# First norm of an AdaLN block without transposes: paired statistics, rows spread through DRAM, product on GpSimd, join on VectorE

## The reference

```
mod = (silu(c) @ wmod).reshape(16, 6, 1, 256)            # sa, ca, ga, sb, cb, gb
h  = layernorm(x) * (1 + ca) + sa                          # first norm, over channels
x  = x + ga' * attention(h)                                # a state-space layer
h  = layernorm(x) * (1 + cb) + sb                          # second norm
x  = x + gb' * feedforward(h)

attention: u, gate = split(h @ W_in.T);  b = u @ W_state.T
           dt = min(softplus(u @ W_dt.T + b_dt), 10);  decay = exp(-dt * rate)
           s[t] = decay[t] * s[t-1] + (1 - decay[t]) * b[t]
           out = ((s @ W_C.T) * silu(gate) + h * D) @ W_out.T
feedforward: xr, xk = mixes of h and h shifted by one token
           out = sigmoid(xr @ W_r.T) * (relu(xk @ W_k.T) ** 2 @ W_v.T)
```

## Time and profile before

| | |
|---|---|
| runs (device time) | 361.68 us median of 3 (361.56 to 362.54) |
| span of the profiled execution, first to last instruction | 360.2 us |
| TensorE matmul busy | 353.1 us (98%) |
| TensorE weight load busy | 277.3 us (77%) |
| ScalarE busy | 306.8 us (85%) |
| VectorE busy | 302.7 us (84%) |
| GpSimd busy | 256.5 us (71%) |
| granted TensorE clock | 0.9 or more of full speed in all 40 slices |
| HBM traffic | 20.40 MB read, 8.39 MB written, 80 GB/s over the span |

### The profile page before, as it was taken

How to read it: one execution, slowest core, us unless ns; L and a number is a source line. 1 busy time by engine, 2 the same in 40 slices (tenths; PEclk the granted TensorE clock), 3 DMA queues, 4 the chain that set the end, 5 groups by cost and what they waited for, 6 DMA issues and landing times.

```text
span 360.2 us, 5599 instructions
## 1 busy us (share of the span) xinstructions
PE 353.1 (98%) x1680; PEld 277.3 (77%) x1680; DVE 302.7 (84%) x640; ACT 306.8 (85%) x422; POOL 256.5 (71%) x268
## 2 busy tenths in 40 slices
PE   8999899999999999999999999999999999999995
PEld 4667567788888888888888888888888888887654
DVE  3779997989989798988979898997989789768846
ACT  4677689799898989989898998989898998988484
POOL 2140849969696987969697796969789696766642
PEclk9999999999999999999999999999999999999999
DMA  8932130220413132040313104031301103010013
GB/s 289 405 119 70 46 119 0 88 90 0 136 40 116 59 104 74 13 146 18 118 60 116 60 35 139 4 116 59 119 0 58 61 0 118 0 61 1 0 58 117
DMA packets 13150, 29.15 MB, mean 81 GB/s; under 512 B 1216, under 2 KB 1984, under 8 KB 12992
## 3 DMA queue, kind: packets, MB, share of 16 engines
q1 hardware_dynamic: 12400, 28.32, 22.6%
q10 hardware_dynamic: 720, 0.48, 0.4%
HBM read 20.40 MB, written 8.39 MB: 80 GB/s over the span
## 4 chain that ended last, share of the span: by engine, by line
PE 91%; DVE 4%; ACT 2%; issue 2%; POOL 0%; ACTq 0%; DVEq 0%; POOLq 0%
PE slot L259 70%; PE slot L266 7%; PE slot L355 4%; PE slot L510 2%; PE slot L509 2%; PE slot L519 2%; PE slot L280 1%; PE slot L273 1%; ACT prev L636 1%; PE slot L363 1%; DVE xn L901 1%; PE slot L302 0%; DVE xk L935 0%; DVE stats L858 0%; DVE xr L935 0%
## 5 line engine op out<-in xcount | busy, mean ns | idle before, releaser
L1147 POOL TENSOR_TENSOR rstd<-mv,half_neg 128x4 f32<-128x4 f32 x16 | 16.1, 1009 | 44.8 <-DVE mv L873 44.8
L636 ACT ACTIVATE prev<-slot,mod,mix_prev 128x512 f32<-128x512 f32 x64 | 46.5, 790 | 1.1 <-PE slot L266 0.8
L259 PE MATMUL slot<-h_hi,wf_hi 128*128 128x512 f32 x120 | 44.0, 407 | 0.0
L1123 POOL TENSOR_TENSOR k_lo<-k_act,k_hi 128x512 fp32r<-128x512 f32 x30 | 38.2, 1297 | 7.7 <-ACT k_act L839 4.2
L1123 POOL TENSOR_TENSOR xk_lo<-xk,xk_hi 128x512 fp32r<-128x512 f32 x30 | 38.4, 1299 | 6.3 <-ACT xk_hi L664 6.3
L259 PE MATMUL slot<-h_hi,wf_lo 128*128 128x512 f32 x120 | 42.8, 397 | 0.0
L1166 POOL TENSOR_TENSOR h_lo<-h,h_hi 128x512 fp32r<-128x512 f32 x28 | 35.8, 1301 | 9.7 <-ACT h_hi L645 9.7
L1123 POOL TENSOR_TENSOR xr_lo<-xr,xr_hi 128x512 fp32r<-128x512 f32 x32 | 42.3, 1324 | 0.2 <-ACT xr_hi L670 0.2
L1217 POOL TENSOR_TENSOR z_lo<-z,z_hi 128x512 fp32r<-128x512 f32 x26 | 33.7, 1298 | 4.9 <-ACT z_hi L738 4.7
L957 DVE TENSOR_TENSOR slot<-silu,slot 128x1024 f32<-128x1024 f32 x16 | 19.7, 1230 | 20.0 <-PE slot L519 18.8
L259 PE MATMUL slot<-h_lo,wf_hi 128*128 128x512 f32 x120 | 35.1, 397 | 0.0
(11 more groups left out here) (157 smaller groups left out, 1009.7 us busy)
## 6 DMA issues: line engine op xcount, KB each, us to landing
x_ch<-x_ch_in SPq DMA_DIRECT2D x16, 512.0 KB, 3.8
x_tok<-x_tok_in SPq DMA_DIRECT2D x15, 512.0 KB, 3.5
x_out<-wmod SPq DMA_DIRECT2D x15, 512.0 KB, 3.0
wmod<-wmod_in SPq DMA_DIRECT2D x1, 1024.0 KB, 8.8
w_in<-weights_in SPq DMA_DIRECT2D x1, 1024.0 KB, 11.5
w_in<-weights_in SPq DMA_DIRECT2D x1, 512.0 KB, 4.5
wmod<-wmod_in SPq DMA_DIRECT2D x1, 512.0 KB, 5.7
x_tok<-x_tok_in SPq DMA_DIRECT2D x1, 256.0 KB, 3.2
```

What stands on the lines that cost most here:

```text
L259: ins = nc.tensor.matmul(out, w[:, c, at + d * P:at + (d + 1) * P], x[:, c, :], start=first, stop=last)
L636: return nc.scalar.activation(prev[:, mix, i, 1:T + 1], ps_n[:, i, :], ACT.Identity, bias=mod_at(SHIFT2 + i, k), scale=mix_prev[:, mix, i, ...
L1123: nc.gpsimd.tensor_tensor(lo, x, hi.bitcast(F32), ALU.subtract).then_inc(done, 1)
L1147: nc.gpsimd.tensor_tensor(rstd2[:, k % 2], mv2[:, k % 2, 1, :], half_neg[:], ALU.pow).then_inc(rstd2_ok, 1)
```

## The change

It touches the first norm from the fourth batch on (k = 3 to 15, 13 batches); batches 0 to 2 stay as they were. With r(t) and m(t) the reciprocal deviation and mean of token t, the modulated norm is written as

h = (x * r) * (1 + ca) + (sa - (1 + ca) * m * r)

with channels on partitions all through, so that nothing is transposed:
- The host lays out `x_tok` of these batches as pairs of tokens with interleaved channels. One `bn_stats` of 512 elements gives the statistics of its even and of its odd elements, that is of two tokens: two instructions in place of four, and no `bn_aggr`.
- GpSimd makes two rows from them (`ln1_rows`): r/sqrt(C), and the mean times it; the factor sqrt(C) is put into `scale_root` and `scale_neg` once.
- SyncE writes the rows (2 x 512 numbers) to DRAM, waits for that, and reads them back with every partition getting both rows (`spread_rows`, 512 KB in SBUF, two buffers).
- GpSimd multiplies `x_ch` by the first row, two halves (`scaled`), into the memory of `xn1` (`scaled1`, one buffer).
- ScalarE makes the offset from the second row (`offsets`), two halves.
- VectorE joins the two into `h` (`modulated`), a step earlier than ScalarE did before.

The diff, cut:

```diff
@@ memory @@
+        scaled1 = xn1[:].rearrange("p a b -> p (a b)").rearrange("p (c t) -> p c t", c=CH)
+        rows1 = sb("rows1", [P, 2, 2, TT])
+        spread_rows = sb("spread_rows", [P, 2, 2, T])
+        offset1 = sb("offset1", [P, CH, T])
+        rows1_d = nc.dram_tensor("rows1_spread", [NB, 2, T], F32).ap()
@@ SyncE @@
+            def spread(k):
+                sp.wait_ge(rows_ok, k - WHOLE)
+                sp.dma_start(rows1_d[k].rearrange("h (p j) -> p h j", j=TT), rows1[:, k % 2]).then_inc(s_row_out, 16)
+                sp.wait_ge(s_row_out, 16 * (k - WHOLE))
+                if k - 2 > WHOLE:
+                    sp.wait_ge(offset_ok, k - 2 - WHOLE)
+                    sp.wait_ge(scaled1_ok[1], k - 2 - WHOLE)
+                sp.dma_start(spread_rows[:, k % 2], rows1_d[k].partition_broadcast(P)).then_inc(s_row_in[k % 2], 16)
@@ SyncE, steps @@
                 if live(a + 3) and live(a):
-                    sp.wait_ge(xn1a_ok, a + 1)
-                    sp.wait_ge(xn1b_ok, a + 1)
+                    if a <= WHOLE:
+                        sp.wait_ge(xn1a_ok, a + 1)
+                        sp.wait_ge(xn1b_ok, a + 1)
+                    else:
+                        sp.wait_ge(st1_ok, a + 1)
                     load_tokens(a + 3)
+                if live(a + 1) and a + 1 > WHOLE:
+                    spread(a + 1)
@@ TensorE @@
                 if live(b) and b > WHOLE:
+                    pe.wait_ge(z_ok[0], b)
+                    pe.wait_ge(z_ok[1], b)
                     pe.wait_ge(hhi_ok, b)
...
-                if live(a):
-                    first_norm(a)
@@ ScalarE @@
+            def offsets(k):
+                act.wait_ge(s_row_in[k % 2], 16 * ((k - WHOLE + 1) // 2))
+                act.wait_ge(root_ok, 1)
+                if k > WHOLE + 1:
+                    act.wait_ge(h_ok, k)
+                for i in range(CH):
+                    last = nc.scalar.activation(offset1[:, i], spread_rows[:, k % 2, SHIFT], ACT.Identity,
+                                                bias=mod_at(SHIFT1 + i, k), scale=scale_neg[:, i, k:k + 1])
+                last.then_inc(offset_ok, 1)
...
                 if live(b) and b > WHOLE:
-                    act.wait_ge(t1_ps, b + 1)
-                    act.wait_ge(z_ok[0], b - 1)
-                    act.wait_ge(z_ok[1], b - 1)
-                    modulated(b, 0)
                 if 0 < d < LAST:
                     rounded_xk(d, 1)
                 if live(b) and b > WHOLE:
-                    modulated(b, 1).then_inc(h_ok, 1)
                     rounded_h(b)
...
+                if live(a):
+                    offsets(a)
                 if live(b):
                     if b > WHOLE:
                         exponential(b)
...
-                if live(a) and a > WHOLE + 1:
-                    ln1_apply(a)
@@ VectorE @@
+            def ln1_rows(k):
...
+                for q in range(TT // 2):
...
+                    last = nc.vector.bn_stats(stats1[:, k % 2, q, :], x_tok[:, k % 3, 2 * q:2 * q + 2].rearrange("p a b -> p (a b)"))
+                last.then_inc(st1_ok, 1)
+            def modulated(k):
+                dve.wait_ge(offset_ok, k - WHOLE)
+                for i in range(CH):
+                    dve.wait_ge(scaled1_ok[i], k - WHOLE)
+                    last = nc.vector.scalar_tensor_tensor(h[:, k % 2, i], scaled1[:, i], scale_root[:, i, k:k + 1], offset1[:, i], ALU.mult, ALU.add)
+                last.then_inc(h_ok, 1)
...
                     normalised(c)
+                if live(a):
+                    modulated(a)
                 if live(b):
                     gated(b)
...
-                    ln1_stats(a + 2)
+                    ln1_rows(a + 2)
...
-                if live(a + 2):
-                    ln1_mean_variance(a + 2)
...
-                if live(a + 1):
-                    ln1_apply(a + 1)
@@ GpSimd @@
+            def ln1_rows(k):
+                pool.wait_ge(st1_ok, k + 1)
...
+                nc.gpsimd.tensor_tensor(rows1[:, k % 2, RSTD], spread1[:, k % 2, 1, :], half_neg[:], ALU.pow).then_inc(row_rstd_ok, 1)
...
+            def scaled(k):
+                pool.wait_ge(s_row_in[k % 2], 16 * ((k - WHOLE + 1) // 2))
+                pool.wait_ge(s_xc[k % 2], 16 * (k // 2 + 1))
+                pool.wait_ge(h_ok, k)
+                for i in range(CH):
+                    nc.gpsimd.tensor_tensor(scaled1[:, i], x_ch[:, k % 2, i], spread_rows[:, k % 2, RSTD], ALU.mult).then_inc(scaled1_ok[i], 1)
...
                     low_part(xr_lo[:, 0], xr[:, 0], xr_hi[:, 0], xrhi_ok[0], r_ps, xrlo_ok[0], d)
+                if live(a):
+                    scaled(a)
                 if b == WHOLE:
                     low_state(b)
...
-                if live(a + 1) and d > 0:
-                    ln1_scale(a + 1)
+                if live(a + 1):
+                    ln1_rows(a + 1)
```

More of the change, by code:

```diff
@@ L85, in adaln_block @@
         xn1 = sb("xn1", [P, TT, C])
+        scaled1 = xn1[:].rearrange("p a b -> p (a b)").rearrange("p (c t) -> p c t", c=CH)
+        rows1 = sb("rows1", [P, 2, 2, TT])
+        spread_rows = sb("spread_rows", [P, 2, 2, T])
+        offset1 = sb("offset1", [P, CH, T])
+        scale_root = sb("scale_root", [P, CH, NB])
+        scale_neg = sb("scale_neg", [P, CH, NB])
+        rows1_d = nc.dram_tensor("rows1_spread", [NB, 2, T], F32).ap()
+        RSTD, SHIFT = 0, 1
         stats2 = sb("stats2", [P, 2, TT, 6])
@@ L158, in adaln_block @@
         s_xc = sems("x_ch_in", 2)
+        s_row_out, s_row_in = sem("rows1_out"), sems("rows1_in", 2)
         s_out = sems("x2_out", 2)
@@ L896, in ln1_apply @@
                 last.then_inc(xn1b_ok, 1)
+            def ln1_rows(k):
+                before(dve, rows_ok, k - 2 - WHOLE)
+                for q in range(TT // 2):
+                    if q == 0:
+                        dve.wait_ge(s_xt[k % 3], 16 * (k // 3 + 1))
+                    last = nc.vector.bn_stats(stats1[:, k % 2, q, :], x_tok[:, k % 3, 2 * q:2 * q + 2].rearrange("p a b -> p (a b)"))
[6 more added lines that the diff above has]
+                last.then_inc(h_ok, 1)
             def ln2_apply(k, tiles, done):
@@ L1036, in _ @@
             clipped(1)
-            ln1_stats(3)
+            ln1_rows(3)
             after_attention(0)
@@ L1044, in _ @@
             normalised(0)
-            ln1_stats(4)
-            ln1_apply(3)
+            ln1_rows(4)
             mixing(0, 0)
@@ L1135, in ln1_scale @@
                 nc.gpsimd.tensor_tensor(shift1[:, k % 2], spread1[:, k % 2, 0, :], rstd1[:, k % 2], ALU.mult).then_inc(shift1_ok, 1)
+            def ln1_rows(k):
+                pool.wait_ge(st1_ok, k + 1)
+                tokens = stats1[:, k % 2, 0:TT // 2, :].rearrange("p q (e s) -> p (q e) s", s=3)
+                nc.gpsimd.tensor_scalar(spread1[:, k % 2, 1, :], tokens[:, :, 2], EPS * C, None, ALU.add).then_inc(row_spread_ok, 1)
+                if k - 2 > WHOLE:
+                    pool.wait_ge(s_row_out, 16 * (k - 2 - WHOLE))
+                pool.wait_ge(row_spread_ok, k - WHOLE)
+                nc.gpsimd.tensor_tensor(rows1[:, k % 2, RSTD], spread1[:, k % 2, 1, :], half_neg[:], ALU.pow).then_inc(row_rstd_ok, 1)
+                pool.wait_ge(row_rstd_ok, k - WHOLE)
+                nc.gpsimd.tensor_tensor(rows1[:, k % 2, SHIFT], tokens[:, :, 1], rows1[:, k % 2, RSTD], ALU.mult).then_inc(rows_ok, 1)
             def weight_low_part(n, at):
@@ L1169, in _ @@
             ln1_scale(1)
+            pool.wait_ge(mod1_ok, 1)
+            nc.gpsimd.tensor_scalar(scale_neg[:], mod[:, SCALE1:SCALE1 + CH, :], -float(np.sqrt(C)), None, ALU.mult)
+            nc.gpsimd.tensor_scalar(scale_root[:], mod[:, SCALE1:SCALE1 + CH, :], float(np.sqrt(C)), None, ALU.mult).then_inc(root_ok, 1)
             weight_low_part(1, MIX_K)
@@ L1174, in _ @@
             second_scale(0)
-            ln1_scale(3)
+            ln1_rows(3)
             weight_low_part(3, MIX_V)
@@ L1231 @@
     x = np.ascontiguousarray(a["x"])
+    tiles = x.reshape(x.shape[0], -1, P, C).transpose(0, 2, 1, 3)
+    pairs = x.reshape(x.shape[0], P, -1, 2, C).transpose(0, 1, 2, 4, 3).reshape(tiles.shape)
     arrays = {
-        "x_tok": np.ascontiguousarray(x.reshape(x.shape[0], -1, P, C).transpose(0, 2, 1, 3)),
+        "x_tok": np.ascontiguousarray(np.concatenate([tiles[:3], pairs[3:]])),
         "x_ch": np.ascontiguousarray(x.transpose(0, 2, 1)),
```

11 lines of the change are left out of this document (2 added, 9 removed).

## The result

Over four runs each the changed kernel took 386.62 us (386.29 to 387.12), the kernel before 362.11 (361.56 to 363.27): a ratio of 1.066, 95% interval 1.063 to 1.069. Slower, as forecast, but by 24.5 us and not by 8.2, and outside the range.

What follows compares the result with a forecast made beforehand. TensorE's chain, 20.83 us a batch, was to give way to a 21.45 us loop between residuals through the x_ch load. Start +2.0 and ten rounds +6.2 made +8.2 on 361.68: 369.9 us, range 361.5 to 377.

Steps and rivals of the forecast that it cites:

- Transposes, 0.87 a batch if TensorE stays the limit: On TensorE, eight first-norm transposes fewer in each of 13 batches: 0.87 us each time, 11.3 us in all.
- rival (b): GpSimd's wait for x_ch is absorbed and the kernel gets faster, 358.5 or 352.4 us; chance 0.13.
- Product 2.52 us, between 0 and 2.8: On GpSimd, the added pair of 128x512 products per batch, priced like a pair of same-shape subtractions there.
- The product waits for x_ch, landing 3.9: GpSimd's products wait for their batch's x_ch load, issued after the residual two batches earlier and landing 3.9 us later.
- Loop 21.45: Residual to residual through x_ch's load, GpSimd, TensorE, ScalarE and VectorE: 21.45 us a batch, 0.62 more than 20.83.
- The signs I named for it: Products idle 2.5 us for x_ch, TensorE a microsecond before state_lo; residuals 21.4 us apart; TensorE's share under 95%.
- Start +2.0: In step 3 the products delay state_lo and TensorE by 2.4 us, VectorE gives 0.4 back: +2.0 us.
- Last rounds and tail at nothing: The last two rounds, with no statistics left to take, and the unchanged tail add no time.
- Small instructions at nothing: On GpSimd, the row statistics' small instructions replace four by three; the difference was costed at nothing.
- (a): Rival: x_ch's load takes 4.6 us in company, rounds 22.15 us, total 376.9 us; chance 0.09.
- (c): Rival: loop and old step meet, with landing 3.3 us or half-price products; 361 to 363.5 us; chance 0.06.
- (d): Rival: the rows through DRAM come late, deciding beyond 10.5 us for both transfers; 380 us at 11.5; chance 0.02.

Runs made afterwards that it cites:

- e3: The changed kernel with the second norm's five small VectorE instructions replaced, for batches 2 to 14, by four aggregates and one addition: 375.92 us, 1.038 of the kernel before.
- e2: The changed kernel without the GpSimd products, VectorE's join reading x_ch itself (result not the reference's): 361.01 us, 0.996 of the kernel before.
- f3: e2 with ScalarE's square of k moved ahead of the rounding of the state, on two x_ch buffers: 358.39 us, 0.988 of the kernel before.
- e1: The changed kernel with a third x_ch buffer, so its load is issued a batch earlier: 370.02 us, 1.022 of the kernel before.
- e6: e1 with the exponential left in PSUM for the clip to read, and ScalarE's square ahead of the rounding of the state: 364.29 us, 1.006 of the kernel before.
- b2: The kernel before plus, in 12 steps, an unread GpSimd product of one SBUF tile and a constant: 367.03 us, 1.014 of the kernel before.
- b1: The kernel before plus, in 12 steps, an unread GpSimd product of two SBUF tiles beside the mv instructions: 375.55 us, 1.037 of the kernel before.
- e7: e6 with GpSimd's row instructions moved behind k_lo: 368.67 us, 1.016 of the kernel before.
- e9: e1 with the square first, batch 3's offsets early, and the products on VectorE ahead of the clip, none on GpSimd: 365.45 us, 1.006 of the kernel before.

## Why the prediction was right or wrong

**The sign was right, two of its steps were not, and one of them carries the error.** The sign isn't luck: e3 shows that the loop of the prediction by itself makes the kernel slower (1.038). But it isn't what the changed kernel was slow by.

- *Transposes, 0.87 a batch if TensorE stays the limit.* It doesn't: e2 gives 0.13 a batch. Something near the "0.4 of the 0.87" in rival (b), 0.32, is what f3 gives, and only with the square moved. I had priced one branch beneath TensorE (z_hi) and not the chain through scan, state_hi and five ScalarE instructions, on which that branch hangs.
- *Product 2.52 us, between 0 and 2.8.* As work, right: 2.54. **This is the step that failed all the same**: the sum asked what the product takes on GpSimd and what waits behind it there, and left VectorE out: it put at nothing what the product does to the instructions that run beside it. That price is 1.1 us for each product that a small VectorE instruction in the chain starts beside, two a round. 20.70 + 1.93 (1.12 + 1.15, less twice 0.17) is 22.63, and 22.67 was measured.
- *The product waits for x_ch, landing 3.9.* Right: it waits 12 times, 27.0 us in all and 2.8 at most, and over the span the landing is 3.7 in the median. The load also sets the time at which product and mv meet: with a third buffer the round falls to 21.26.
- *Loop 21.45.* It is there, 21.83 in e3, but a longer one lies over it. (The 375 given for a landing of 4.3 with the join dear doesn't follow from its terms: 0.4 and 0.55 more a round make some 379.) The signs I named for it fell accordingly: residuals are 22.67 apart and not 21.4, and TensorE waits not for state_lo but for state_hi, 1.64 us at 195.39. TensorE's share under 95% and the product's wait of about 2.5 came as said.
- *Start +2.0.* It is +3.0. state_lo of step 3 starts at 57.69, as forecast (57.75), but takes 1.72 in place of 1.30 beside VectorE's join, and the gate product comes 2.9 later (60.23 against 57.35): the same omission, 0.4 us of it. The 0.4 that VectorE was to give back isn't seen.
- *Last rounds and tail at nothing.* +3.2. The residuals' loop does end there, but it wasn't the one that limits, and the products go on to batch 15.
- *Small instructions at nothing.* Nothing by their own length, dear by their place: the mv instructions in the chain of VectorE, the rows' on GpSimd (2.3 us between state_lo and k_lo, e6).
- *Rivals.* (a) landing 4.6: no, 3.7. (b) and (c), wait absorbed: even with no wait at all (e1) the kernel is 2.2% slower. (d) rows late: no; the spread is issued at 200.68, lands 4.1 us later in the median, and is read by ScalarE's offsets at 207.67 and by GpSimd at 212.61.

The Trainium skill has the rule that I didn't weigh (SBUF — State Buffer, SBUF: two separate sides; also GPSIMD Engine Reference, Specifications): VectorE instructions with two SBUF inputs, or in a mode that uses two ports, share a port pair with GpSimd, and whichever starts first has it for its whole instruction. The trace agrees, with 1.28 us in place of 0.15 beside a product, and 0.38 for four aggregates that have one input; b2 differs, where the held instruction took 0.61 of the dummy's 1.51. The clip and e3's addition, one input each, were held too; whether they ran in a mode of two ports no run here shows.

## What to carry to other kernels

When work is moved to GpSimd, list VectorE's instructions that run in the same microseconds and read two SBUF tiles, or go from SBUF to SBUF with one input like the clip here, whatever their size: if one is on the chain of waits, the moved work is paid there, up to its full length. A min/median/max of an instruction in the trace of before often has the price already (0.998 against 0.166 here); read the outliers. And an engine that is "the bound" at 98% may have the next chain only 0.13 us a batch beneath it, so price the removal of its work by that chain.

## What the runs showed of the hardware

- A VectorE instruction of 4 numbers per partition with two SBUF inputs takes 1.1 to 1.3 us instead of 0.16 when it starts just after a GpSimd product of 128x512 (1.29); it ends within 0.04 us of the product (the changed kernel, b1).
- Held as well: SBUF to SBUF with one input, the clip (0.99 for 0.43) and a 128x4 addition (0.66). Not held: aggregates (0.38 for four), the clip from PSUM (0.69, its own price with or without), and the driven input and the scan, whose second tensor is in PSUM (0.68 beside a product in e3, 1.22).
- GpSimd is held too, by VectorE's join (k_lo's pair 3.03 for 2.54 in e7; a 128x4 scaling of the row statistics 0.68 beside the join, 0.24 in e7, where it comes later) and by products there (xr_lo 1.74 for 1.30, e9).
- A GpSimd instruction with one input holds its neighbour for a part only: the neighbour took 0.61 (0.16 unheld) beside one of 1.51 (b2).
